# The eight transposes of a tap, dealt out in pairs between the fp32 matmuls of the tap before

## What is computed

```python
om = conv(gn(x), w_off) + b_off                      # 27 maps
sampled = vmap(_bilinear)(gn(x), ys, xs) * sigmoid(mask)
x = x + einsum('bckhw,ock->bohw', sampled, w_conv)   # layer 0
out1 = relu(batchnorm(conv3x3(gn(x), ternary(w1))))
x = x + relu(out1 + batchnorm(conv3x3(out1, ternary(w2))))
```

## Time and profile before

| | us |
|---|---|
| median of 3 runs | 3144.83 |
| lowest and highest run | 3138.27, 3150.94 |
| span of the profiled execution | 3182.4 |
| TensorE busy in the span | 2628.3 (83%) |
| DVE, POOL, ACT busy | 2230.3, 1718.6, 1220.3 |

### The profile page before, as it was taken

How to read it: one execution, slowest core, us unless ns; L and a number is a source line. 1 busy time by engine, 2 the same in 40 slices (tenths; PEclk the granted TensorE clock), 3 DMA queues, 4 the chain that set the end, 5 groups by cost and what they waited for, 6 DMA issues and landing times. The chain is left out here.

```text
span 3182.4 us, 39166 instructions
## 1 busy us (share of the span) xinstructions
PE 2628.3 (83%) x11674; PEld 1747.1 (55%) x11674; DVE 2230.3 (70%) x5146; ACT 1220.3 (38%) x2103; POOL 1718.6 (54%) x1294
## 2 busy tenths in 40 slices
PE   4768788879999999899999989989898969999500
PEld 2434444445555656565555555555555759999500
DVE  5478787887778888877777777777775255565544
ACT  1234444444444444444444344444442123233244
POOL 1057677765666676566676667767771013333111
PEclk9788999999999999999999999999999989999755
DMA  5589999997898999888898888988884121111387
GB/s 170 161 291 343 330 329 322 351 358 276 306 333 314 341 336 331 307 286 308 315 329 306 310 312 304 326 306 328 325 317 153 60 68 57 51 53 57 116 272 245
DMA packets 286846, 827.49 MB, mean 260 GB/s; under 512 B 26204, under 2 KB 59996, under 8 KB 285924
## 3 DMA queue, kind: packets, MB, share of 16 engines
q0 software_dynamic: 170496, 620.83, 54.0%
q1 hardware_dynamic: 116196, 204.94, 19.4%
HBM read 740.19 MB, written 85.48 MB: 259 GB/s over the span
## 5 line engine op out<-in xcount | busy, mean ns | idle before, releaser
L359 POOL DMA_INDIRECT G<-pixel_pairs,quad_c x1152 | 1532.4, 1330 | 683.3 <-PE psT L781 328.4
L645 DVE SCALAR_TENSOR_TENSOR G<-G,wts_c 128x256 f32<-128x256 f32 x3456 | 1399.5, 479 | 315.2 <-ACT G L407 250.1
L744 PE MATMUL psD<-ST,wconv 128*128 128x512 f32 x2304 | 1072.2, 612 | 0.0
L744 PEld LDWEIGHTS psD<-ST,wconv 128*128 128x128 f32 x2304 | 436.5, 199 | 454.0 <-issue 454.0
L407 ACT ACTIVATE G<-G,wts_c 128x256 f32<-128x256 f32 x1152 | 524.0, 503 | 421.3 <-DMA G<-pixel_pairs,quad_c 351.3
L733 PE MATMUL psF<-pf,qw 128*128 128x512 f32 x2304 | 631.5, 423 | 14.9 <-DVE pf L569 7.9
L781 PE MATMUL psT<-idn,G 128*128 128x128 f32 x2304 | 332.2, 291 | 233.7 <-DVE G L645 224.3
L733 PEld LDWEIGHTS psF<-pf,qw 128*128 128x128 f32 x2304 | 429.3, 189 | 164.1 <-issue 54.7
L781 PEld LDWEIGHTS psT<-idn,G 128*128 128x128 f32 x2304 | 280.1, 149 | 322.0 <-issue 169.6
L444 ACT ACTIVATE ST<-psT 128x1024 f32<-128x1024 f32 x288 | 292.8, 1017 | 269.7 <-PE psT L781 247.3
L733 PE MATMUL psA<-po,woff 128*64 128x512 f32 x1152 | 345.2, 447 | 6.3 <-DVE po L569 6.3
(11 more groups left out here) (136 smaller groups left out, 1609.2 us busy)
## 6 DMA issues: line engine op xcount, KB each, us to landing
pixel_pairs<-yT SPq DMA_DIRECT2D x112, 256.0 KB
G<-pixel_pairs,quad_c POOLq DMA_INDIRECT x1152
xz<-in_x SPq DMA_DIRECT2D x32, 512.0 KB
xres<-in_x SPq DMA_DIRECT2D x32, 512.0 KB
x<-x1c SPq DMA_DIRECT2D x32, 512.0 KB
h<-h1c SPq DMA_DIRECT2D x32, 512.0 KB
area<-h SPq DMA_DIRECT2D x32, 512.0 KB, 6.9
area<-x SPq DMA_DIRECT2D x32, 512.0 KB, 5.2
```

The source lines that it names most:

```text
L359: pool.indirect_dma_start(out=G[:, i % RING, :], out_offset=None, in_=tbl[d.b].rearrange("y x q c -> (y x) (q c)"), in_offset=bass.Indirec ...
L645: dve.scalar_tensor_tensor(g[:, 0:C], g[:, q * C:(q + 1) * C], wts_c[:, d.p, q * NG + i:q * NG + i + 1], g[:, 0:C], ALU.mult, ALU.add).the ...
L744: ins = pe.matmul(psD[:, oc, :], wconv[:, t, k, oc * 128:(oc + 1) * 128], ST[:, k % 3, t, :], start=(k == 0 and t == 0), stop=(k == TAPS - ...
```

## The change

On TensorE alone. The transposes of tap k and the four matmuls of tap k-1 are issued alternately: the pair of tile 0, one matmul, the pair of tile 1, one matmul, and so on. Each pair waits for the third multiply-add of its own tile. The wait for the evacuation of tap k-1, which both the transposes and the matmuls need, stands ahead of all of them. `d_tr` is still given by the eighth transpose, which now has three matmuls ahead of it. Tap 0 of a chunk has no matmuls to alternate with, and tap 8's four matmuls follow at the end of the chunk as before.

```diff
+                def deform_ready(d, k):
                     pe.wait_ge(d_st, TAPS * d.n + k + 1)
                     if k == 0:
                         need(pe, d_x1, d.n + CREDIT)
...
+                def deform_piece(k, piece):
+                    oc, t = piece // CT, piece % CT
+                    return pe.matmul(psD[:, oc, :], wconv[:, t, k, oc * 128:(oc + 1) * 128], ST[:, k % 3, t, :],
+                                     start=(k == 0 and t == 0), stop=(k == TAPS - 1 and t == CT - 1))
+
+                def turn_sampled(d, k, t):
+                    pe.wait_ge(d_mac, 3 * NG * d.n + 3 * PT * k + 2 * PT + t + 1 + CREDIT)
+                    for c in range(CT):
+                        ins = pe.transpose(psT[:, c, t * 128:(t + 1) * 128],
+                                           G[:, (PT * k + t) % RING, c * 128:(c + 1) * 128], idn[:])
+                    return ins
...
                         if d:
-                            need(pe, d_mac, 3 * NG * d.n + 3 * PT * (k + 1) + CREDIT)
                             need(pe, d_st, TAPS * d.n + k)
+                            if k > 0:
+                                deform_ready(d, k - 1)
                             for t in range(PT):
-                                for c in range(CT):
-                                    ins = pe.transpose(psT[:, c, t * 128:(t + 1) * 128],
-                                                       G[:, (PT * k + t) % RING, c * 128:(c + 1) * 128], idn[:])
-                            ins.then_inc(d_tr, 1)
+                                ins = turn_sampled(d, k, t)
+                                if t == PT - 1:
+                                    ins.then_inc(d_tr, 1)
+                                if k > 0:
+                                    ins = deform_piece(k - 1, t)
                             if k > 0:
-                                deform_tap(d, k - 1)
+                                ins.then_inc(d_conv, 1)
...
                     if d:
-                        deform_tap(d, TAPS - 1)
+                        deform_ready(d, TAPS - 1)
+                        for piece in range(CT * CT):
+                            ins = deform_piece(TAPS - 1, piece)
+                        ins.then_inc(d_conv, 1)
```

More of the change, by code:

```diff
@@ L736, in conv_tap @@
                     return ins
-                def deform_tap(d, k):
+                def deform_ready(d, k):
                     pe.wait_ge(d_st, TAPS * d.n + k + 1)
```

## The result

After: 3156.84 us, the median of 15 runs (3145.77 to 3166.5). Before, in the same comparison: 3142.88 us, 15 runs (3135.99 to 3153.26). The ratio is 1.0046, with an interval of 1.0033 to 1.0059: 14 us slower, just inside the half per cent that the forecast took for what a measurement can tell.

What follows compares the result with a forecast made beforehand. No engine was full; a ring of transposes, POOL gathers and ACT/DVE weighting was taken to bind. Chunk ends +14 and +6, POOL stalls -18 made +2 us, carried to the median: 3146 us, range 3080 to 3215.

Steps and rivals of the forecast that it cites:

- TensorE's own work: Transposes and matmuls of every tap: pairs stay 0.22 us, matmuls 0.86, a tap 4.32; no difference taken.
- the ends of -92 and +184 us: Limits for TensorE's own work: pairs at 0.14 us return at most 92; pairs costing their whole 0.38 lose 184.
- rival 4: Interleaved pairs cost their whole 0.38 us, half of it on TensorE's path: +92, 3238 us; alone 0.05.
- The end of a chunk: Tap 8's later release delays the next chunk: +14 us in stages 1 to 3, +6 in stage 0.
- The stalls of POOL, -18: Tap 6's delayed gathers break DVE's run in stages 1 and 2; five tap 7 waits shrink from 4.40 to 0.75 us.
- the difference is carried over: The +2 us sum on the profiled span of 3182.4 us is applied to the runs' median of 3144.8, giving 3146.
- stands until the run breaks: A POOL gather begun well into an unbroken DVE run stands until that run breaks; one took 9.09 us.
- The other waits, at taps 3 to 8, I leave at nothing: TensorE's remaining waits at taps 3 to 8 were given no gain or loss in the sum.
- The 1.2 of the start and the 1.4 of the later release meet three taps on: Reason for zero at taps 3 to 8: starts 1.2 us sooner offset releases 1.4 us later.
- Rival 1: Tap 3's fourth gather stops stalling in five stage 0 chunks, 6.0 us each: -30, 3116 us; chance 0.33 together with Rival 2.
- Rival 2: TensorE's 97 waits shorten by 1.2 us each, nothing given back: 116 us, 3030 us; alone 0.05.
- Rival 3: Delayed gathers of taps 6 and 7 stall in eleven more chunks, 5.4 us each: 3223 us; 0.30 with rival 4.

Runs made afterwards that it cites:

- tap 8 alone: Kernel before with only tap 8's transposes interleaved with tap 7's matmuls, with waits per tile there and the old wait elsewhere; 3206.83 us, ratio 1.0142.
- waits alone: Kernel before with its order kept (eight transposes, then four matmuls), but each pair waiting for its own tile; 3110.55 us, ratio 0.9836.
- tap 8 in the old order: The change, but with tap 8's eight transposes ahead of tap 7's four matmuls again; taps 1 to 7 interleaved; 3125.45 us, ratio 0.9874.
- tap 1 alone: Kernel before with a wait for each tile and only tap 1 interleaved; 3078.93 us, ratio 0.9788; run again, 3087.23 us, ratio 0.9797.
- tap 3 alone: Kernel before with only tap 3 interleaved and one wait for the whole tap everywhere; 3180.44 us, ratio 1.0125.
- The last comparison: Wait per tile, all taps but 3 and 8 interleaved, 3107.07 us, ratio 0.9855; beside it only tap 1 interleaved, 3087.23 us, ratio 0.9797.

## Why the forecast came out as it did

The forecast, 3146 us and no change, was 11 us under the median. It came out in part by luck, as terms that cancel: of its steps one was too large, and two were wrong.

**TensorE's own work: right.** The steps of 0.22 and 0.86 stand unchanged in the timeline after; neither of the ends of -92 and +184 us came, so rival 4 (a pair that costs its whole 0.38) fell.

**The end of a chunk: right in its steps, too large in its sum.** In the chunk shown every step came within 0.15 us of the working: DVE at X + 5.19 (forecast 5.33), its end at 10.03 (10.17), tap 0's transposes at 8.99 (about 9.0), tap 1's at 16.19 (16.25). The new idle time ahead of tap 8's matmuls is 0.25 us, 8.1 us over the span (forecast 0.4). The row behind tap 0's matmuls starts 0.48 later than before (forecast 0.57). The versions give this term a scale. "Change x 32" takes every chunk for one like that shown. "All ends" adds up, over the 31 chunks that another follows, the time from X to the start of the last pass of tap 0's matmuls in the traces; it is given against 671, the mean of the two profiles of before (669 and 674), and two profiles of one version differ in it by 2 to 10 us.

| version | behind X, us | change x 32 | all ends, us | measured, us |
|---|---|---|---|---|
| before | 19.65 | | | |
| the change | 20.13 | +15 | +6 and -5 | +14 |
| tap 8 alone | 21.37 | +55 | +42 | +45 |
| waits alone | 18.97 | -22 | -32 | -52 |
| tap 8 in the old order | 18.91 | -24 | -36 | -40 |
| tap 1 alone | 18.52 | -36 | -45 and -47 | -67 |

(Measured: the ratio less one, times 3143.) Tap 1's dealing out, on top of the waits alone, is 14 by the chunk shown, 13 to 15 by all ends and 15 in the runs. Tap 8's is 42 of the 45 us that it cost alone, and 31 to 41 of the 54 in a kernel that has the rest. So the chunk's end carries most of tap 8's price. The change as a whole stands at +6 and -5 there, where the forecast had +14 and +6. What makes its profiles shorter lies between the ends, from tap 0's matmuls to the transposes of tap 8: 1495 and 1477 us before, 1456 and 1464 after.

**The stalls of POOL, -18, and "the difference is carried over" to the median: the step that failed.** In the profiles the mechanism came in the main as written. The delayed gathers starve DVE, its run breaks, the 9 us gather of the earlier trace rows is gone and the waits of 4.4 at tap 7 are below 1.2. The profiles even gave more: from the first transpose of stage 1 to that of stage 3 the kernel before took 1167.2 us, 1147.3 in its second profile, and the kernel after 1136.7. What failed is the carrying over. The two profiles of the change are 21 to 29 us shorter than the two of before, and in the runs it is 14 and 12 us slower. An execution that is profiled is one of many: the 14 profiled here lie between 14 us under the median of their runs and 39 over it (1.7 added to the span of before), so one profile cannot price a step of 20 us.

Whether median executions have the stalls stays open. Without the term the sum is +20, so 3165, and with it 3146; the measured 3157 lies between, and its interval, 10 to 19 us over before, shuts out both. Both profiles of before are long for their runs, by 39 and 17 us, and contain the stalls, so a gain may exist in long executions alone. That is argued: a run without a profile leaves no trace, and the second profile came out as the sign that the stalls are ordinary. What the runs do show is that their end was no gain by itself: with tap 3 alone they went, and the kernel was 39 us slower.

The Trainium skill ("SBUF — State Buffer", section "SBUF: two separate sides") has a DVE instruction with two SBUF inputs hold the shared ports for that instruction. The trace does not agree: behind the five waits gathers stood 8.4 to 9.2 us in the first profile of before and 6.8 to 7.6 in the second, across many instructions of 0.40. Two readings of the forecast were off. The gather of 3.27 us in the earlier trace rows begins 3.6 us into DVE's run and ends 2.8 before the run does, so "stands until the run breaks" does not hold for all. And the lower clock behind the earlier trace rows did not come in the idle time: the granted clock was 1.00 in 1434.00:1439.50, idle but for its first 1.15 us, and 0.66 on average in 1439.55:1441.10, with TensorE busy again, so it fell to the lower level only behind the wait.

**"The other waits, at taps 3 to 8, I leave at nothing": wrong twice, in opposite directions.** The wait for each tile gave 52 us, 20 more than its share of the chunk's end by all ends (32), 30 more by the chunk shown (22). The later release at taps 2 to 7 took 27 back. That these nearly cancel is luck. From version to version the runs go -52 for the waits, -15 for tap 1's order, +27 for taps 2 to 7 and +54 for tap 8's; these steps lead from before to the change, so they make +14 by themselves and prove nothing by it. "The 1.2 of the start and the 1.4 of the later release meet three taps on" treated a tap as one that gains both ways; where no tap waits the start gains nothing, and the later release is felt all the same. The last comparison puts that in stage 0.

**Rival 1** (the fourth gather of tap 3 passes in stage 0) came true, without the price. After, in stage 0:

```profile
522.30 1.02 ACT L444 ACTIVATE ST<-psT 128x1024 f32<-128x1024 f32 x1 [6.20 <-PE psT L751]
...
523.83 4.89 DVE L645 SCALAR_TENSOR_TENSOR G<-G,wts_c 128x256 f32<-128x256 f32 x12 [2.17 <-ACT G L407]
...
527.68 1.54 PE L751 MATMUL psT<-idn,G 128*128 128x128 f32 x8 [0.61 <-DVE G L645]
...
531.10 9.57 DVE L645 SCALAR_TENSOR_TENSOR G<-G,wts_c 128x256 f32<-128x256 f32 x24
...
533.92 1.23 POOL L359 DMA_INDIRECT G<-pixel_pairs,quad_c  x1 [0.30 <-issue]
```

It begins 2.8 us into DVE's run and takes 1.23, where the earlier trace rows have 7.22. Of the gathers of tap 3, 19 and 20 stood for over 5 us in the two profiles of before, five of the 19 in stage 0; in those of the change it was 5 and 1. At the forecast's 6.0 each that is 84 us and more. The waits alone leave seven such gathers and gain 52 us in all, less than the 72 of twelve: a gather that stands is not 6.0 us on the path. Stage 0 is 528 us long in the profile after as in the second of before: over the span POOL's time in gathers is 1337 us after, 1522 in that second profile, and its wait for the transposes 542 instead of 349. What gain there was lies within those 52 us. **Rival 2** (all waits shorten, nothing is given back, 3030) has its half in the waits alone: the waits were real, at 52 us and not 116, and they were given back. **Rival 3** (delayed gathers stall in chunks that had none) came in small, as waits of 0.75, where tap 3 alone was dealt out with the old wait. Its price of 5.4 was a little low besides: the wait and clock of the earlier trace rows make 4.40 + 1.28 = 5.7. In the change no wait at tap 7 of stages 1 and 2 is over 1.2.

What stays open: by what path the late releases of taps 2 to 7 cost, tap 3's 39 us above all, how many stalls a median execution has, and which part of the profiles' gain the median lacks.

## What to carry to other kernels

Split a change that does two things before pricing it: the finer wait was worth 1.6% alone, the new order cost 3.0% alone, and together they showed as 0.4%. Dealing work out between the parts of a producer paid where the consumer stood waiting, as at tap 1 (3078.93 us, the best version here). At the other taps it delayed the release behind the last part and cost time: 45 us at tap 8, whose release is on the path into the next chunk, 39 at tap 3, whose path was not found, and some 18, with wide intervals, at the five others together. And where the profiled execution lies above the runs, an event seen in it may be what makes it so: the price of removing that event should not be carried over to the median in full.

## What was not expected of the hardware

How far into an unbroken run of DVE a gather begins does not decide whether it stands. In the kernel after, the gather above that began 2.82 us into a run (533.92 against 531.10) took 1.23 us, past the 2.44 that the forecast took for a margin; this one, in stage 1, began 2.83 us into a run and stood 7.62 (timeline):

```profile
808.02 9.63 DVE L645 SCALAR_TENSOR_TENSOR G<-G,wts_c 128x256 f32<-128x256 f32 x24
...
810.85 7.62 POOL L359 DMA_INDIRECT G<-pixel_pairs,quad_c  x1 [0.30 <-issue]
```

In the kernel before one begun 2.38 us into a run of 24 stood 8.02 (at 1168.98), and one begun 5.23 us into a run of 27 passed in 1.22. What decides was not found.

Switching TensorE between pairs of fp32 transposes and fp32 matmuls eight times a tap costs nothing that the trace shows: the steps are the same 0.22 and 0.86 us as in closed groups.
